# Where a graph network's second layer gets its transposed onehots: turned on TensorE, or compared from keys broadcast by DMA

## The chip, the cores and the metric

One core of a Trainium2 chip runs the whole program. The metric is the device time of one launch in microseconds, without a profile, as a median of several runs.

## What is computed

Two message-passing layers on 12500 nodes with 64 features and 212500 edges, sorted by dst:

```python
h = jnp.maximum(_layernorm(x, axis=-1), 0.0)
x = x + segment_sum(h[src] @ weight[etype], dst)            # layer 0, 16 relations
h = jnp.maximum(_layernorm(x, axis=-1), 0.0)
pre = concatenate([h[src], h[dst], edge_attr]) @ W1 + b1
x = x + segment_sum(relu(pre) @ W2 + b2, dst)               # layer 1
```

All of it is fp32. The text calls the first of these the first layer, the second the second layer.

## The kernel before, in words

The edges are cut into G = 208 groups of 1024, a group into T = 8 tiles of 128 edges. Since dst is sorted, the edges of one tile fall on few neighbouring nodes (at most W0 = 16), those of a group into a window of 128 nodes. A kernel-side test picks a slower path for edge lists where that isn't so; here the fast path runs.

**Gathers.** Either layer needs one table row per edge. POOL issues one indirect DMA per tile (`gather`, L711), 128 rows of 64 numbers each, 8 per group: from x and h_table in the first layer, from p_table in the second. p_table holds every node's h times its part of W1 for src, q_table the same for dst, with b1; both are written during the first layer. POOL's program is an order of its own: it waits once per half-round for the index list `idx`, and before each group until `pre_added` says that the rows of the group two before have been summed.

**Matrices of zeros and ones.** `key1[edge, tile]` is an edge's dst less the first dst of its tile (0 to 15), `key_w[slot]` the place of a slot (tile, offset) in the group's window of nodes. DVE makes, four groups (half a round, B = 4) at a time, `oh1` (edge by slot: `make_onehots`, L1171) and `placer` (slot by node: `make_placers`, L1176), each by one comparison with a row of numbers. The second layer also needs both transposed: `oh1_t` (slot by edge) and `placer_t` (node by slot). Before the change PE turns them (`turn_onehots`, L1394, four transpositions at a time into the PSUM bank `turn_ps`) and ACT copies them to SBUF (`copy_onehots`, L923).

**One group of the second layer.** SP loads a window of q rows (L644). PE picks for each slot its node's q row with placer_t (`pick_q`, L1401), DVE spreads it by tile (`spread_q`, L1211), PE multiplies the edge features by their part of W1 (L1406) and adds oh1_t times q (L1407), DVE adds the gathered p rows (`add_rows`, L1187, which signals `pre_added`), ACT takes the relu (L927), PE sums edges into slots with oh1 (`sum_group`, L1411), DVE keeps each tile's own block and reduces (L1194, L1198), PE places slots into nodes with placer (`place_z`, L1415), and DVE adds that to the accumulator (L1207). `count_edges` (L1182) counts the edges of each slot from oh1_t. The edge features are turned on PE too (`turn_attr`, L1390), which the change leaves as it is.

**Order of the work.** Every engine runs a program written out by hand: a round of U = 8 steps, one group each, in a loop of NIT = 26 rounds. In step u, PE does the products of group u−1, the placement of u−3, the sum of u−2 and the pick of u; DVE the corresponding parts. In steps 1 and 5 DVE makes the onehots of the next half-round, in 2 and 6 the placers; PE turns the onehots in steps 2 and 6 and the placers in 3 and 7; DVE counts in 3 and 7. In step 6 PE also multiplies a finished chunk of nodes by W2 (L1380). SP, in `pairs`, loads q windows for two groups after every second group, and after every fourth the next half-round's `idx` (L637) and edge features `attr` (L628), whose innermost runs are 32 bytes.

**Before the loops.** DVE makes the keys by edge group (`key1_g`, 104 partitions by 2 × 1024) and the places (`head_f`) at 75 to 77 us; PE turns them to the form by edge. The accumulator `acc` lies where the edge lists and `key1_g` lay, and is cleared when they have been read (L1112 to L1114).

## Time and profile before

| | |
|---|---|
| time, median of 3 runs (lowest, highest) | 4229.12 us (4224.97, 4232.71) |
| the profiled execution: its span (the page gives no other time of it) | 5160.7 us |
| POOL busy in the profiled span | 61% |
| PE, DVE, ACT busy | 53%, 29%, 11% |
| granted TensorE clock, mean | 0.681 |
| DMA moved | 144 MB, 28 GB/s |

The execution under the profiler is some 930 us longer than those that are timed. An instruction's duration can be read from it; a wait has to be asked whether it exists without the profiler. The second layer runs from about 2635 us to the end.

### The profile page before, as it was taken

Reading aid. Unit: us, or ns where it says so; the run is one execution under the profiler, and the core shown is the slowest. Engines: PE = TensorE matmul, PEld = TensorE weight load, DVE = VectorE, ACT = ScalarE, POOL = GpSimd, SP = SyncE. Lnnn points to the kernel's source line nnn. Section 1 sums busy time; section 2 is a strip of 40 time slices with the busy share of each in tenths; the row PEclk is TensorE's granted clock in tenths of the full one; section 3 lists DMA queues with packets and bytes.
Section 4 is the critical chain, followed back from the end, with each engine's and each line's share of the span. In section 5 each row is a group of like instructions: output and inputs, shape, how many; then the busy total and the mean of one; then the engine's idle time right before and its main releaser. Section 6 shows DMA issues by size and latency. Waiting matters only on the chain.

```text
span 5160.7 us, 36581 instructions
## 1 busy us (share of the span) xinstructions
PE 2728.2 (53%) x10312; PEld 1524.6 (30%) x10312; DVE 1473.2 (29%) x2000; ACT 582.7 (11%) x1138; POOL 3161.4 (61%) x3350
## 2 busy tenths in 40 slices
PE   2655555555555555455555455554454554554555
PEld 1433333333333333333332222222222222222222
DVE  6322222222222222222233233233232333232232
ACT  3111111111111111111110000010000010000010
POOL 7466565566666566656646566665665666665665
PEclk9776677776767667676766666666666666666666
DMA  4111111111111111111111111111111111111111
GB/s 95 21 24 23 23 26 23 23 26 24 24 25 24 23 24 26 24 23 25 24 27 30 27 29 28 30 30 26 31 29 26 31 30 28 29 29 26 31 29 26
DMA packets 392815, 144.34 MB, mean 28 GB/s; under 512 B 323186, under 2 KB 338859, under 8 KB 392795
## 3 DMA queue, kind: packets, MB, share of 16 engines
q0 software_dynamic: 106496, 109.26, 11.1%
q1 hardware_dynamic: 283685, 34.22, 4.6%
q10 hardware_dynamic: 2614, 0.62, 0.1%
q8 instruction: 8, 0.13, 0.0%
q14 instruction: 12, 0.10, 0.0%
HBM read 129.23 MB, written 12.83 MB: 28 GB/s over the span
## 4 chain that ended last, share of the span: by engine, by line
another core or an unknown queue 33%; PE 24%; issue 21%; POOL 9%; DVE 7%; DVEq 1%; DMA 1%; ACT 1%; SPq 1%; POOLq 0%; ACTq 0%
POOL rows L711 9%; PE ps L1333 7%; PE ps L1407 5%; PE ps L1406 4%; PE ps L1411 2%; DVE q_blk L1211 2%; DVE z_slot L1198 2%; PE ps L1347 2%; PE ps L1340 1%; DVE slots L1187 1%; DVEq L1202 1%; DMA rows<-h_table,idx 1%; PE ps L1306 1%; PE ps L1307 1%
## 5 line engine op out<-in xcount | busy, mean ns | idle before, releaser
L711 POOL DMA_INDIRECT rows<-p_table,idx x1664 | 1574.4, 946 | 959.7 <-issue 527.3
L711 POOL DMA_INDIRECT rows<-h_table,idx x1616 | 1528.2, 946 | 999.0 <-issue 461.4
L1406 PE MATMUL ps<-w_attr,attr_t 64*128 64x512 f32 x416 | 363.2, 968 | 1156.8 <-DVE q_blk L1211 873.1
L1333 PE MATMUL ps<-onehot,rows 128*64 128x256 f32 x3328 | 704.9, 555 | 455.1 <-DMA rows<-h_table,idx 371.2
L1060 DVE TENSOR_TENSOR onehot<-key,ps 128x2048 f32<-128x2048 f32 x209 | 474.1, 2276 | 556.6 <-remote 439.7
L1333 PEld LDWEIGHTS ps<-onehot,rows 128*64 128x64 f32 x3328 | 355.4, 196 | 728.5 <-issue 663.4
L1340 PE MATMUL ps<-w_types,slots 128*128 128x128 f32 x3328 | 455.5, 294 | 96.3 <-issue 78.5
L1340 PEld LDWEIGHTS ps<-w_types,slots 128*128 128x128 f32 x3328 | 424.4, 207 | 151.9 <-issue 131.0
L1187 DVE TENSOR_TENSOR slots<-ps,rows 128x512 f32<-128x512 f32 x208 | 143.9, 692 | 1052.9 <-remote 438.9
L1406 PEld LDWEIGHTS ps<-w_attr,attr_t 64*128 64x128 f32 x416 | 85.9, 256 | 1195.7 <-issue 1195.7
L1407 PE MATMUL ps<-q_blk,onehot 128*128 128x512 f32 x416 | 411.0, 1090 | 0.0
L877 ACT COPY slots<-ps 128x512 f32<-128x512 f32 x416 | 239.9, 587 | 1001.1 <-PE ps L1333 470.4
L1411 PE MATMUL ps<-relus,onehot 128*128 128x512 f32 x416 | 341.3, 918 | 0.0
L927 ACT ACTIVATE relus<-slots 128x512 f32<-128x512 f32 x208 | 131.0, 630 | 1429.8 <-DVE slots L1187 1008.7
L1194 DVE TENSOR_TENSOR z_blk<-ps,blocks 128x512 f32<-128x512 f32 x208 | 143.7, 691 | 494.7 <-remote 280.4
L1347 PE MATMUL ps<-place,nodes_t 128*64 128x256 f32 x416 | 155.3, 513 | 174.5 <-ACT nodes_t L881 138.7
L1127 DVE TENSOR_TENSOR acc<-acc,ps 64x128 f32 x208 | 58.2, 280 | 642.8 <-PE ps L1347 366.3
L1198 DVE TENSOR_REDUCE z_slot<-z_blk 128x64 f32<-128x512 f32 x208 | 208.7, 1003 | 0.0
L1211 DVE TENSOR_TENSOR q_blk<-ps,blocks 128x512 f32<-128x512 f32 x208 | 141.6, 681 | 215.2 <-remote 160.9
L1295 PE MATMUL ps<-ident,stage 64*120 64x64 f32 (+1 forms) x104 | 18.1, 322 | 329.1 <-ACT stage L838 262.2
L1407 PEld LDWEIGHTS ps<-q_blk,onehot 128*128 128x128 f32 x416 | 96.5, 288 | 268.9 <-issue 268.9
L1401 PEld LDWEIGHTS ps<-q_win,onehot 128*128 128x128 f32 x416 | 112.6, 272 | 185.3 <-issue 185.3
(136 smaller groups left out, 1693.0 us busy)
## 6 DMA issues: line engine op xcount, KB each, us to landing
rows<-p_table,idx POOLq DMA_INDIRECT x1664
rows<-h_table,idx POOLq DMA_INDIRECT x1616
attr<-in_edge_attr_dram SPq DMA_DIRECT2D x52, 128.0 KB
q_win<-q_table SPq DMA_DIRECT2D x208, 32.0 KB
p_table<-pq_out SPq DMA_DIRECT2D x25, 120.0 KB
q_table<-pq_out SPq DMA_DIRECT2D x25, 120.0 KB
out_dram<-xs SPq DMA_DIRECT2D x25, 120.0 KB
xs<-in_x_dram SPq DMA_DIRECT2D x6, 480.0 KB, 6.5
```

What stands on the lines that cost most here:

```text
L711: pool.indirect_dma_start(rows[:, u, t, :], None, table, bass.IndirectOffsetOnAxis(ap=idx[:, u, t:t + 1], axis=0)).then_inc(s, 16)
L877: act.copy(to, slot_ps[:, u % 2, t, :].rearrange("p t (r w) -> p t r w", w=W0)).then_inc(slots_copied, 1)
L1060: dve.tensor_tensor(onehot[:, b], key0[:, bass.ds(g, 1), :].rearrange("p a (t c) -> p (a t) c", c=1).broadcast_to([P, T, C0]), iota_ps.rea ...
L1187: dve.tensor_tensor(presum[:, u % 2, 0:T * D], pre_ps[:, u % 2, :], rows[:, u].rearrange("p t d -> p (t d)"), ALU.add).then_inc(pre_added, 1)
L1198: dve.tensor_reduce(z_slot[:, u, 0:D], z_blk[:].rearrange("p (t d) -> p d t", d=D), X, ALU.add).then_inc(z_slotted, 1)
L1211: dve.tensor_tensor(by_tile(q_blk[:, u % 2, :]), q_ps.rearrange("p (a d) -> p a d", a=1).broadcast_to([P, T, D]), own_tile, ALU.mult).then ...
L1333: last = pe.matmul(slot_ps[t % 2 * D:(t % 2 + 1) * D, b, t // 2, :], rows[:, u, t, :], onehot[:, b, t, :], start=True, stop=True)
L1340: last = pe.matmul(nodes_ps, slots[:, b, r, :], w_types[:, r, :], start=(r == 0), stop=(r == R - 1))
L1347: last = pe.matmul(win_ps, nodes_t[:, h * D:(h + 1) * D], place[:, h, :], start=(h == 0), stop=(h == 1))
L1406: pe.matmul(pre_ps[:, u % 2, :], attr_t[half, u // 2, :], w_attr[half].rearrange("k j d -> k (j d)"), start=True, stop=False)
L1407: pe.matmul(pre_ps[:, u % 2, :], oh1_t[:, u, :], q_blk[:, u % 2, :], start=False, stop=True).then_inc(pre_made, 1)
L1411: pe.matmul(z_ps, oh1[:, u, :], relu_rows[:, u % 2, :], start=True, stop=True).then_inc(z_made, 1)
```

## The change

The transposed matrices of the second layer are no longer turned. Early in the first layer SP stores the keys (`key1_g`) and the places (`head_f`) to two new tables in DRAM, `key_rows` and `head_rows`, by nine DMAs, and DVE waits for these before it clears the accumulator. In the second layer SP's new `load_keys` loads for each half-round the four groups' keys straight into `oh1_t`, each tile's row repeated on its 16 partitions, and the places into `placer_t`, repeated on all 128: 256 KB each. These loads count on `attr_in`, as the features do, so each wait for the features (48 in place of 16) is a wait for all three. DVE then compares in place: `oh1_t` with the partition's number modulo 16, `placer_t` with the partition's number (`of_part`, made at the start by an iota on POOL and two small DVE instructions). The semaphore `masks_turned` takes the place of `onehots_copied`, PE and ACT lose the turns and copies, and PE's waits for `onehot1` and `placer1` move to the first use of oh1 and placer in each half-round.

```diff
         SROWS = P * (-(-(N + P) // P))
+        key_rows = dram("key_rows", (G // B, T, B, P), fp32)
+        head_rows = dram("head_rows", (G, P), fp32)
         sums0 = dram("sums0", (SROWS, KA), fp32)
...
         eps = sb("eps", [P, 1], fp32)
+        of_part = sb("of_part", [P, 2], fp32)
+        of_part_i = sb("of_part_i", [P, 2], i32)
         zrows = sb("zrows", [P, D], fp32)
...
         z_ps = ps[:, 2, :]
-        turn_ps = ps[:, 3, :]
         q_ps = ps[:, 4, 0:D]
...
         placer1 = sem("placer1")
-        onehots_turned = sem("onehots_turned")
-        onehots_copied = sem("onehots_copied")
+        tables_stored = sem("tables_stored")
+        masks_turned = sem("masks_turned")
         q_picked = sem("q_picked")
...
                     sp.dma_start(idx[:, u, :], src_tab[:, u, :]).then_inc(idx_in[u], 16)
+                sp.wait_ge(heads_spread, 1)
+                sp.wait_ge(keys_made, 2)
+                for a in range(2):
+                    for b in range(B):
+                        sp.dma_start(key_rows[a * HG // B:(a + 1) * HG // B, :, b, :],
+                                     key1_g[b:HG:B, a, :].rearrange("g (t e) -> g t e", t=T)).then_inc(tables_stored, 16)
+                sp.dma_start(head_rows.rearrange("(a g) e -> g a e", a=2), head_f[:]).then_inc(tables_stored, 16)
...
+                def load_keys(m, k):
+                    of_tile = key_rows[bass.ds(m, 1)].rearrange("n t b e -> t n (b e)").broadcast_to([T, W0, B * P])
+                    sp.dma_start(oh1_t[:, k * B:(k + 1) * B, :].rearrange("p u e -> p (u e)"), of_tile).then_inc(attr_in[k], 16)
+                    of_slot = head_rows[bass.ds(m * B, B), :].rearrange("(a g) s -> a (g s)", a=1).broadcast_to([P, B * P])
+                    sp.dma_start(placer_t[:, k * B:(k + 1) * B, :].rearrange("p u s -> p (u s)"), of_slot).then_inc(attr_in[k], 16)
+
                 def load_idx(g, k):
...
                             if ahead:
+                                load_keys((it + 1) * 2 + k, k)
                                 load_idx((it + 1) * U + k * B, k)
+                            else:
+                                load_keys(0, k)
                             if ahead == 1 and k == U // B - 1:
...
+                sp.wait_ge(tables_stored, 16 * (2 * B + 1))
                 for k in range(U // B):
+                    load_keys(k, k)
                     load_attr(k * B, k)
...
             pool.iota(by_first(slot_row_i[:]), pattern=[[P, 2], [1, P // 2]], base=0, channel_multiplier=0).then_inc(consts_made, 1)
-            pool.wait_ge(consts_made, 10)
+            pool.iota(of_part_i[:], pattern=[[0, 2]], base=0, channel_multiplier=1).then_inc(consts_made, 1)
+            pool.wait_ge(consts_made, 11)
...
-                def copy_onehots(to, n, k):
-                    act.wait_ge(onehots_turned, n)
-                    act.copy(to[:, k * B:(k + 1) * B, :].rearrange("p u c -> p (u c)"), turn_ps).then_inc(onehots_copied, 1)
-
                 def copy_relu(it, u):
...
                         copy_attr(*on(it, u, 2))
-                    if u % B == 2:
-                        copy_onehots(oh1_t, it * 4 + u // B * 2 + 3, (u // B + 1) % 2)
-                    if u % B == 3:
-                        copy_onehots(placer_t, it * 4 + u // B * 2 + 4, (u // B + 1) % 2)
                 copy_attr(0, 0)
-                copy_onehots(oh1_t, 1, 0)
-                copy_onehots(placer_t, 2, 0)
                 for u in range(U):
...
                 tmp, tmp2 = head_rel[:], stat_a[0:HG, NK - 1, 1, 0:2]
-                dve.wait_ge(consts_made, 10)
+                dve.wait_ge(consts_made, 11)
                 chain(dve.tensor_single_scalar(limit_i[:], limit_i[:], U.bit_length() - 1, ALU.arith_shift_right))
...
                     make_onehot0(k - NA - 1, (k - NA - 1) % 2)
+            dve.wait_ge(consts_made, 11)
+            chain(dve.tensor_single_scalar(of_part_i[:, 0:1], of_part_i[:, 0:1], W0 - 1, ALU.bitwise_and))
+            dve.tensor_copy(of_part[:], of_part_i[:])
             chain(dve.tensor_single_scalar(slot_row_i[:], slot_row_i[:], P + W0 - 1, ALU.bitwise_and))
...
                 dve.sem_inc(window_added, AHEAD)
+                dve.wait_ge(tables_stored, 16 * (2 * B + 1))
                 dve.memset(acc[:, 2 * 2 * GE:3 * 2 * GE], 0.0)
...
+                def turn_onehots(n, k):
+                    half = oh1_t[:, k * B:(k + 1) * B, :]
+                    dve.wait_ge(attr_in[k], 48 * n)
+                    dve.tensor_scalar(half, half, of_part[:, 0:1], None, ALU.is_equal).then_inc(masks_turned, 1)
+
+                def turn_placers(k):
+                    half = placer_t[:, k * B:(k + 1) * B, :]
+                    dve.tensor_scalar(half, half, of_part[:, 1:2], None, ALU.is_equal).then_inc(masks_turned, 1)
+
                 def count_edges(n, k):
-                    dve.wait_ge(onehots_copied, n)
+                    dve.wait_ge(masks_turned, n)
                     dve.tensor_reduce(z_slot[:, k * B:(k + 1) * B, D], oh1_t[:, k * B:(k + 1) * B, :], X, ALU.add)
...
                         make_placers(m, k)
+                        turn_onehots(it + 1 + u // B, k)
                     if u % B == 3:
+                        turn_placers(k)
                         count_edges(it * 4 + u // B * 2 + 3, k)
...
                 dve.memset(acc[:], 0.0).then_inc(z_added, AHEAD)
+                turn_onehots(1, 0)
+                turn_placers(0)
                 for u in range(U):
...
                     if u % B == 0:
-                        wait_apart(pe, attr_in[u // B], 16 * (it + 1))
+                        wait_apart(pe, attr_in[u // B], 48 * (it + 1))
                     if not first:
...
-                def turn_onehots(v, k):
-                    for b in range(B):
-                        last = pe.transpose(turn_ps[:, b * P:(b + 1) * P], v[:, k * B + b, :], ident[:])
-                    last.then_inc(onehots_turned, 1)
-
                 def pick_q(it, u):
                     if u % B == 0:
-                        wait_apart(pe, onehots_copied, it * 4 + u // B * 2 + 2)
+                        wait_apart(pe, masks_turned, it * 4 + u // B * 2 + 2)
                     pe.wait_ge(q_in[u % V], 16 * (it * (U // V) + u // V + 1))
...
                     half = slice(u % 2 * T * F, (u % 2 + 1) * T * F)
+                    if u % B == 0:
+                        wait_apart(pe, masks_turned, it * 4 + u // B * 2 + 1)
                     wait_apart(pe, q_spread, it * U + u + 1)
...
                 def sum_group(it, u):
+                    if u % B == 0:
+                        wait_apart(pe, onehot1, it * 2 + u // B + 1)
                     pe.wait_ge(relu_made, AHEAD + it * U + u + 1)
...
                 def place_z(it, u):
+                    if u % B == 0:
+                        wait_apart(pe, placer1, it * 2 + u // B + 1)
                     pe.wait_ge(z_slotted, it * U + u + 1)
...
                         turn_attr(*on(it, u, 2))
-                    k = (u // B + 1) % 2
-                    if u % B == 2:
-                        wait_apart(pe, onehot1, it * 2 + u // B + 2)
-                        turn_onehots(oh1, k)
-                    if u % B == 3:
-                        wait_apart(pe, placer1, it * 2 + u // B + 2)
-                        wait_apart(pe, onehots_copied, it * 4 + u // B * 2 + 3)
-                        turn_onehots(placer, k)
...
                 turn_attr(0, 0, first=True)
-                pe.wait_ge(onehot1, 1)
-                turn_onehots(oh1, 0)
-                pe.wait_ge(placer1, 1)
-                pe.wait_ge(onehots_copied, 1)
-                turn_onehots(placer, 0)
                 for u in range(U):
...
```

## Rows read from the trace of the kernel before

**Rows 1.** the page, parts 1 and 5: busy time by engine, and POOL's gathers
```profile
PE 2728.2 (53%) x10312; PEld 1524.6 (30%) x10312; DVE 1473.2 (29%) x2000; ACT 582.7 (11%) x1138; POOL 3161.4 (61%) x3350
...
L711 POOL DMA_INDIRECT rows<-p_table,idx x1664 | 1574.4, 946 | 959.7 <-issue 527.3
L711 POOL DMA_INDIRECT rows<-h_table,idx x1616 | 1528.2, 946 | 999.0 <-issue 461.4
```

**Rows 2.** line 711 alone: gathers (ns min/median/max), and idle time before them
```profile
L711 POOL DMA_INDIRECT rows<-p_table,idx x1664: 938/944/1478, 2635.5 to 5134.2; - x185
...
  issue: 1002.9, 3128
  DVE slots L1187: 432.3, 79
  PE ps L1333: 303.1, 46
  remote: 208.6, 71
  DMA idx<-src_tab: 25.8, 3
```

**Rows 3.** timeline of POOL, second layer: start us, us, what, idle before
```profile
3902.44 0.94 POOL L711 DMA_INDIRECT rows<-p_table,idx  x1 [0.30 <-issue]
3903.69 0.94 POOL L711 DMA_INDIRECT rows<-p_table,idx  x1 [0.30 <-issue]
```

**Rows 4.** timeline, SP, PE and ACT around one stall of the second layer
```profile
3910.92 0.72 SPq L628 DMA_DIRECT2D attr<-in_edge_attr_dram  x1
...
3919.47 0.28 PE L1390 MATMUL ps<-ident,attr 128*128 128x128 f32 x1
...
3924.39 0.63 ACT L927 ACTIVATE relus<-slots 128x512 f32<-128x512 f32 x1 [15.11 <-DVE slots L1187]
...
3937.69 0.27 ACT L919 COPY attr_t<-ps 128x128 f32<-128x128 f32 x1 [12.67 <-remote]
```

**Rows 5.** timeline of PE: first products of two steps, a turn between
```profile
3936.43 2.04 PE L1406 MATMUL ps<-w_attr,attr_t 64*128 64x512 f32 x2 [16.24 <-issue]
...
3942.72 0.88 PE L1394 MATMUL ps<-ident,onehot 128*128 128x128 f32 x4
...
3945.20 1.09 PE L1406 MATMUL ps<-w_attr,attr_t 64*128 64x512 f32 x2 [1.60 <-DVE q_blk L1211]
```

**Rows 6.** timeline, DVE and POOL together, start and second layer
```profile
73.79 0.29 DVE L1049 CAST iota_f<-iota_i 128x256 f32<-128x256 int32 x1
...
74.19 1.60 POOL L711 DMA_INDIRECT rows<-h_table,idx  x1 [0.30 <-issue]
...
74.46 1.22 DVE L1052 CAST acc<-acc 104x2048 f32<-104x2048 int32 x1
...
2651.36 0.68 DVE L1171 TENSOR_TENSOR onehot<-key,iota_f 128x512 f32<-128x512 f32 x1
...
2651.70 1.16 POOL L711 DMA_INDIRECT rows<-p_table,idx  x1 [0.30 <-issue]
```

**Rows 7.** timeline of the start, and SP's queue from 40 to 50 us
```profile
101.60 0.21 DVE L1074 CAST slot_row<-slot_row_i 1x128 f32<-1x128 int32 x1
...
103.21 1.76 DVE L1112 MEMSET acc<- 128x2048 f32 x1 [1.21 <-issue]
...
110.06 0.94 POOL L711 DMA_INDIRECT rows<-h_table,idx  x1 [13.27 <-DMA idx<-src_tab]
...
q1 hardware_dynamic: 2014, 1.48, 54.4%
```

**Rows 8.** timeline at the handover to the second layer
```profile
2635.48 0.94 POOL L711 DMA_INDIRECT rows<-p_table,idx  x1 [34.40 <-issue]
2635.49 2.89 SPq L628 DMA_DIRECT2D attr<-in_edge_attr_dram  x2
...
2643.95 0.66 PE L1401 MATMUL ps<-q_win,onehot 128*128 128x64 f32 x2 [0.77 <-issue]
...
2649.56 0.69 DVE L1187 TENSOR_TENSOR slots<-ps,rows 128x512 f32<-128x512 f32 x1 [4.23 <-PE ps L1407]
...
2655.66 0.94 POOL L711 DMA_INDIRECT rows<-p_table,idx  x1 [0.30 <-issue]
...
2656.87 0.69 DVE L1187 TENSOR_TENSOR slots<-ps,rows 128x512 f32<-128x512 f32 x1 [4.82 <-DMA rows<-p_table,idx]
```


## The prediction

> **What bounds the kernel now.** I read the page first. It shows POOL busy for 61% of the span, ahead of PE and DVE, and nearly all of that is one instruction, the gather of 128 rows [rows 1]. The next question is whether POOL's other 39% is slack, so I read its idle time by releaser [rows 2]. Of the 1973 us, 1002.9 us lie in 3128 pauses of about 0.30 us each, which follow every gather: one gather starts 1.25 us after the one before it (0.94 busy, 0.30 idle) and nothing is waited for between them [rows 3]. So 3328 gathers (1616 and 1664, and 48 from x) take 3328 × 1.247 = 4150 us by themselves, nearly the whole measured 4229.12.
>
> The rest of the idle time is real waiting, but mostly of the profiled execution alone. All idle time before gathers is 1002.9 + 432.3 + 303.1 + 208.6 + 25.8 = 1972.7 us [rows 2]; the pauses of 0.30 take 3328 × 0.30 = 998; the handover between the layers takes 34 (POOL's idle time ahead of the second layer's first gather [rows 8]) and the first wait for an index list 13 [rows 7]. That leaves 927 us of stalls. The profiled span is 5160.7 us (the page gives no other time of that execution), and 5160.7 − 927 = 4233 us, against a median of 4229.12 without a profile. The two agree within 5 us, so I take the stalls as absent from the runs that are timed. Their look fits: after the edge features' DMA of 32-byte rows is issued, a PE transposition recorded at 3919.47 is answered by ACT's copy of it only at 3937.69, with ACT idle for the last 12.67 us of that [rows 4]. Such a delay belongs to no arithmetic. **So the measured kernel is POOL's row of gathers, with a start, a handover and a tail.** A gather waits for the sum of rows two groups before it, so the other engines have to make a group in 8 × 1.247 = 9.98 us on average. The step with a turn of four placers takes PE 8.77 us from one product to the next, even at its lower granted clock [rows 5]. That is below 9.98, and the two groups of room smooth what is above the mean.
>
> **The change, part by part.**
> Removed: 8 PE transpositions and 2 ACT copies per four groups, with their waits. They lie beside the gathers, in the 1.2 us by which the longest ordinary PE step is shorter than POOL's group [rows 5]. Worth 0. The moved PE waits for onehot1 and placer1 are for DVE work made a half-round earlier: 0.
>
> Added on SP and in the DMA queues, steady state: per four groups two broadcasts of 256 KB, 52 times. They are issued between the q loads and the idx and attr loads of the same half. By the nearest stretch, in which SP's queue moved 1.48 MB within 10 us [rows 7], 512 KB take about 3.5 us. DVE now waits in step 2 or 6 for both tables and the features together. SP issues them when a group's rows are added (step 4), DVE asks at the end of step 6, nearly 2.5 groups or 25 us later. SP's issues (some 6 us), the tables (3.5) and the features (below 5) add up to about 15. Cover 10 us; cost 0. If the cover is gone, DVE stands in the wait with the next group's sum of rows queued behind it, and POOL behind that. The idx load behind the tables has four groups before POOL wants it: 0. A gather's landing behind the broadcasts may come up to 3.5 us later; the room for that is 8 us: the last gather of group 1 ends near 2655.4, its rows are added at 2656.87 [rows 8], and POOL would need that only at 2655.66 + 9.98 = 2665.6. Cost 0.
>
> Added at the start: one more iota on POOL ahead of the first gather, 0.2 us. Two small DVE instructions ahead of the chain heads, first product, idx load, gather, for which POOL stands idle at 110.06; at 0.21 us each [rows 7], 0.4 us. Nine stores (0.85 MB of keys, 0.1 MB of heads) go out from about 77, when the keys are made, need some 7 us at the rate above, and are waited for by DVE only ahead of the memset at 103.21 [rows 7]. Cost 0; from above 3.
>
> Added at the handover: SP issues four table loads of 256 KB ahead of the q loads. The first q pick was at 2643.95, the first sum of rows at 2649.56, and POOL asked for it at 2655.66 [rows 8]. 1 MB more in the queue is 6.9 us: sum of rows done at 2649.56 + 6.9 + 0.69 = 2657.2, which is 1.5 us late. From below 0 (the transfers overlap better), from above 4. I take 1.
>
> Added on DVE: 104 compares of 128x512 against one number per partition, both operands in SBUF. DVE has the time (it is busy 29%). A row of before that is nearest is the CAST, which also has one input: 128x256 in 0.29 us, 104x2048 in 1.22 us, so 512 elements take 0.29 + 256 × (0.93 / 1792) = 0.42 us. But these can cost POOL time, and **this is the term that decides**. The trace shows two kinds of collision [rows 6]. DVE's compare with two SBUF inputs runs from 2651.36 to 2652.04; the gather that starts inside it at 2651.70 takes 1.16 us instead of 0.94 and ends 0.82 after the compare. So a gather needs something in its first 0.12 us that the compare holds. And the CAST from 74.46 to 75.68 starts inside a gather, which normally would end at 75.13 and ends at 75.79, 0.11 after the cast: a one-input instruction of this fast kind also holds what a gather needs in its last 0.11 us. At a random phase a 0.42 us instruction costs 0.30² / (2 × 1.247) = 0.036 at the first place and 0.42² / (2 × 1.247) = 0.071 at the second, 0.107 in all, or 11 us for 104. But the phases aren't random, as DVE's steps begin with the landing of a gather. The 104 two-input compares of 0.68 us in this layer would cost 0.56² / (2 × 1.247) × 104 = 13 us at random, and cost 1574.4 − 1664 × 0.944 = 3.6 us [rows 1, 2]. I take about the same share with something added for a POOL that never stands: 5 us. Bounds: 0, and 104 × 0.42 = 44.
>
> The Trainium skill, "SBUF — State Buffer", section "Who interferes with whom", states a rule on just this: a tensor_scalar or a cast in a two-port mode contends with GpSimd's descriptor making, and whichever starts first holds the port pair for its whole length. The rows agree that there is contention, but the cast of 74.46 did not wait for the gather that had begun at 74.19, so the second half of the rule isn't seen. By the rule as written, only compares that begin in the 0.30 us pause would stretch a gather: an estimate of 0.24 × 104 × at most 0.42 = 10 us.
>
> Sum: 0.2 + 0.4 + 1 + 5 = 6.6 us. On the profiled execution's own stall-free sum that is 4233 → 4240; on the median it gives 4229.1 + 6.6, **4236 us**.
>
> **The rivals.**
> *The compares lock POOL out nearly every time* (slower). Same mechanism, larger share: since DVE's order is tied to POOL's landings, the phase may be the bad one in each of the 104. Place: the turned placers and onehots at the ends of steps 2, 3, 6, 7. For it: no row shows this instruction and POOL is never idle in the timed runs. Against it: the present compares pay a quarter of the random price. It decides from a mean of 0.07 us a compare on, (8.5 − 1.6) / 104. Its price is up to 44 us: about 4230 + 40 = 4270.
> *The compares hold nothing* (same). If this form runs in the slow mode with one input, as the reduction and the sums from PSUM do, it costs no gather anything: 4229 + 1.6 = 4231.
> *The tables land late* (slower). If the broadcast, which reads one row for many partitions, moves at a third of the rate above, the 10 us of cover are used up; each us beyond is paid 52 times, 2 us give 104, 4335. Against it: 2 KB rows are longer than those of most loads here.
> *Stalls exist without the profile, and the turns cause part of them* (faster). For it: the mean granted clock is 0.681, and the sixth step, with the turn and the output product, is longer than the others. Against it: the 4233 above leaves no room. If such steps overran by 0.7 us once in each of 26 rounds, 18 us would go and 1.6 come: 4213.
>
> **How the numbers follow.** A measurement of this kernel tells apart about 0.2%, 8.5 us. The forecast has 0.46: sums from 4231 to 4245, of which 0.34 lie within 8.5 us and 0.12 above. The compares hold nothing: 0.12, same. POOL locked out: 0.18, slower. Tables late: 0.10, slower. Turns mattered: 0.14, faster. So faster 0.14, same 0.46, slower 0.40. The range from 4212 to 4272 holds all but the late tables and the outer parts of the first and the last rival.
>
> **What would show it.** Right: POOL's gathers in the second layer still 1.25 us apart; the count of gathers above 0.97 us up, with the new compares beside them; the new compare at 0.42 us; busy of L711's second group up by about 5 us; ACT's and PE's idle time longer by what was removed. Wrong: if DVE is seen idle ahead of the onehots' compare, released by the table's DMA, the tables are late; if the gathers' mean rises above 0.960 us, POOL is locked out; if the time falls by more than 8.5 us with the gathers as before, the stall-free reading of the timed runs is false.

## The result, and the profile after

The changed kernel takes 4257.61 us (median of 4, 4247.39 to 4260.02), the kernel before 4229.41 (median of 4, 4224.97 to 4232.71): a ratio of 1.0060, 95% interval 1.0047 to 1.0072. It is 0.6% slower, by 28 us. Measured once more beside the experiments it was 4247.55 against 4222.29, ratio 1.0058 (1.0044 to 1.0072), so 25 us. The page below is that of the shortest of the first four executions, 4247.39 us; the other three took 4257.51 to 4260.02, none of them was profiled, and what made them 10 us longer stays open.

First the page of the changed kernel, parts 1 and 5. Line numbers have moved: L733 is the gather (L711 of before), L1212 the sum of rows (L1187 of before). In the changed kernel L1187 and L1192 are the older two comparisons, which make the onehots and the placers (L1171 and L1176 of before), and L1199 and L1203 are the new two, for the turned onehots and the turned placers.

```profile
span 4245.6 us, 35885 instructions
...
PE 2586.1 (61%) x9888; PEld 1467.2 (35%) x9888; DVE 1496.0 (35%) x2108; ACT 518.4 (12%) x1032; POOL 3179.3 (75%) x3351
```

```profile
L733 POOL DMA_INDIRECT rows<-p_table,idx x1664 | 1594.1, 958 | 539.8 <-issue 532.6
L733 POOL DMA_INDIRECT rows<-h_table,idx x1616 | 1527.1, 945 | 495.5 <-issue 477.9
...
L1212 DVE TENSOR_TENSOR slots<-ps,rows 128x512 f32<-128x512 f32 x208 | 143.9, 692 | 1321.8 <-DMA rows<-p_table,idx 1311.7
```

The span is 4245.6 us and POOL's two groups of gathers hold 3121 us of it. Their idle time is 539.8 and 495.5, nearly all "issue", the pauses of 0.30 us, against 959.7 and 999.0 in [rows 1]: this execution has none of the stalls of the profile of before. ACT and PE have lost their turns, and nobody gained by it. Of the idle time ahead of DVE's sum of rows, 1311.7 of 1321.8 us are waits for the gathers' landing.

The mean gather of the second layer takes 958 ns, where [rows 1] had 946. The comparisons, by line and form, from 2300 to 4200 us (47 half-rounds; count, busy us, mean ns):

```profile
L1187 DVE TENSOR_TENSOR onehot<-key,iota_f 128x512 f32<-128x512 f32 x47 | 31.6, 672 | 0.0
...
L1199 DVE TENSOR_SCALAR onehot<-onehot,of_part 128x512 f32<-128x512 f32 x47 | 22.4, 476 | 0.0
L1203 DVE TENSOR_SCALAR onehot<-onehot,of_part 128x512 f32<-128x512 f32 x47 | 22.3, 475 | 0.0
```

The new ones take 0.476 us, not the 0.42 worked out from the casts. The start and the handover, on POOL's timeline (start, duration, idle time before):

```profile
98.39 0.94 POOL L733 DMA_INDIRECT rows<-h_table,idx  x1 [3.31 <-DMA idx<-src_tab]
```

```profile
2148.86 0.94 POOL L733 DMA_INDIRECT rows<-p_table,idx  x1 [1.70 <-DVE slots L1212]
```

At the start POOL waits 3.31 us for an index list. The kernel before waits 2.79 there (e10, below):

```profile
98.56 0.94 POOL L711 DMA_INDIRECT rows<-h_table,idx  x1 [2.79 <-DMA idx<-src_tab]
```

But this wait differs by more than that from run to run: it is 2.06 in the changed kernel of e9, and 4.06 in e8, which has nothing of the change. A cost of the start isn't shown. Ahead of the third group of the second layer POOL waits 1.70 us (1.62 in e9), where e10 has only the pause of 0.30: the first sum of rows is late by about what was forecast.

### The profile page after: what moved, and what is told of

It reads as the page before. It is cut to its first block, busy times and chain, and to the rows that moved or that the text cites. A ratio compares the mean times of both kernels' runs of the same rounds, so it can differ in the third digit from the quotient of the medians.

```text
span 4245.6 us, 35885 instructions
## 1 busy us (share of the span) xinstructions
PE 2586.1 (61%) x9888; PEld 1467.2 (35%) x9888; DVE 1496.0 (35%) x2108; ACT 518.4 (12%) x1032; POOL 3179.3 (75%) x3351
## 4 chain that ended last, share of the span: by engine, by line
POOL 62%; issue 27%; PE 4%; DMA 4%; DVE 1%; SPq 1%; POOLq 0%; ACT 0%; ACTq 0%; DVEq 0%
POOL rows L733 62%; PE ps L1362 3%; DMA rows<-h_table,idx 2%; DMA rows<-p_table,idx 1%; DVE slots L1212 0%; SPq L565 0%; PE ps L1369 0%; SPq L542 0%; SPq L546 0%; POOLq L360 0%; DMA q_win<-q_table 0%; PE ps L1433 0%; PE ps L1432 0%; SPq L560 0%; DVE stat_a L1035 0%
## 5 line engine op out<-in xcount | busy, mean ns | idle before, releaser
L733 POOL DMA_INDIRECT rows<-p_table,idx x1664 | 1594.1, 958 | 539.8 <-issue 532.6
L733 POOL DMA_INDIRECT rows<-h_table,idx x1616 | 1527.1, 945 | 495.5 <-issue 477.9
L1362 PE MATMUL ps<-onehot,rows 128*64 128x256 f32 x3328 | 632.1, 544 | 721.5 <-DMA rows<-h_table,idx 721.1
L1432 PE MATMUL ps<-w_attr,attr_t 64*128 64x512 f32 x416 | 403.2, 1069 | 784.3 <-DVE q_blk L1236 784.3
L1212 DVE TENSOR_TENSOR slots<-ps,rows 128x512 f32<-128x512 f32 x208 | 143.9, 692 | 1321.8 <-DMA rows<-p_table,idx 1311.7
L1369 PE MATMUL ps<-w_types,slots 128*128 128x128 f32 x3328 | 442.6, 296 | 0.0
L1433 PE MATMUL ps<-q_blk,onehot 128*128 128x512 f32 x416 | 427.6, 1131 | 0.0
L1432 PEld LDWEIGHTS ps<-w_attr,attr_t 64*128 64x128 f32 x416 | 96.1, 286 | 815.2 <-issue 815.2
L1445 PEld LDWEIGHTS ps<-onehot,z_slot 128*65 128x65 f32 x416 | 96.5, 232 | 240.5 <-issue 232.2
L1445 PE MATMUL ps<-onehot,z_slot 128*65 128x128 f32 x416 | 131.4, 420 | 5.2 <-DVE z_slot L1223 5.2
```

The lines of the kernel that those rows point to most:

```text
L733: pool.indirect_dma_start(rows[:, u, t, :], None, table, bass.IndirectOffsetOnAxis(ap=idx[:, u, t:t + 1], axis=0)).then_inc(s, 16)
L1212: dve.tensor_tensor(presum[:, u % 2, 0:T * D], pre_ps[:, u % 2, :], rows[:, u].rearrange("p t d -> p (t d)"), ALU.add).then_inc(pre_added, 1)
L1362: last = pe.matmul(slot_ps[t % 2 * D:(t % 2 + 1) * D, b, t // 2, :], rows[:, u, t, :], onehot[:, b, t, :], start=True, stop=True)
L1369: last = pe.matmul(nodes_ps, slots[:, b, r, :], w_types[:, r, :], start=(r == 0), stop=(r == R - 1))
L1432: pe.matmul(pre_ps[:, u % 2, :], attr_t[half, u // 2, :], w_attr[half].rearrange("k j d -> k (j d)"), start=True, stop=False)
L1433: pe.matmul(pre_ps[:, u % 2, :], oh1_t[:, u, :], q_blk[:, u % 2, :], start=False, stop=True).then_inc(pre_made, 1)
```

## The experiments

Theory: nothing that was taken away bounded anything, and the 25 to 28 us are gathers stretched by DVE's comparisons. Rival: the stores, the loads and the waits cost it. "The port" is a short name for what a comparison and a gather can't have at the same time; a gather counts as stretched when it takes over 0.97 us in place of 0.944. The eight experiments that are compared with 4222 us were run beside the kernel before in three series, its medians 4222.89 (e5), 4222.29 (e6 to e9) and 4222.37 (e10 to e12).

### e1 to e4: a chip on which the same program takes 5185 us

e1 is the kernel before, unchanged.

> The kernel before, unchanged: how far two programs with the same instructions differ, and whether a second profile has the stalls of the first. If the stalls are the profiler's, the timed ratio is 1.000 and the profile may come out near 4230 us with POOL's gathers 1.25 us apart; their time in the second layer then gives what the two comparisons with two SBUF inputs cost without stalls (3.6 us in the first profile; 9 us in the profile of the change). If the stalls were real, the profiled span stays near 5160 us.

e2 is the change with the comparisons' second operand in PSUM:

```diff
+        part_ps = ps[:, 3, P:P + 2]
...
+                chain(dve.tensor_copy(part_ps, of_part[:]))
                 make_onehots(0, 0)
...
-                    dve.tensor_scalar(half, half, of_part[:, 0:1], None, ALU.is_equal)
+                    dve.tensor_tensor(half, half, part_ps[:, 0:1] (over B and P), ALU.is_equal)
```

> The change, but its two comparisons take the partition's number from PSUM, so that each has one SBUF input and can't run in the fast two-port form. Port theory: they stretch no gather, although each takes 0.69 us in place of 0.48; the time falls by 15 to 25 us from the change's 4257.6, to 4233 to 4242, and the gathers next to them take 0.94 us. Rival, the tables' DMAs or the start cost the 28 us: the time stays at 4255 to 4262.

e3 is the kernel before with the change's stores, loads and waits:

```diff
+                for a in range(2):
+                    for b in range(B):
+                        sp.dma_start(key_rows[...], key1_g[...])
...
+                                load_keys((it + 1) * 2 + k, k)      # into unused columns of presum
                                 load_idx((it + 1) * U + k * B, k)
...
-                        wait_apart(pe, attr_in[u // B], 16 * (it + 1))
+                        wait_apart(pe, attr_in[u // B], 48 * (it + 1))
```

> The kernel before, with all of the change's DMAs and waits (the nine stores, DVE's wait for them, the two 256 KB loads per half-round, into SBUF that nothing reads, PE's wait for them), while the matrices are turned on PE as before. Port theory: 4229 to 4233, at most 3 us for the start and the handover. Rival, DMA: 4250 to 4260.

e4 is the change with each new comparison followed by one more:

```diff
                     dve.tensor_scalar(half, half, of_part[:, 0:1], None, ALU.is_equal).then_inc(masks_turned, 1)
+                    dve.tensor_scalar(unused_b, unused_a, of_part[:, 0:1], None, ALU.is_equal)
```

> The change, with each of its two comparisons followed by a second one of the same form (128x512, one SBUF input, into SBUF that nothing reads), so 208 in place of 104. Port theory: the pair takes some 0.88 us in a row, and an instruction that starts in it or ends in it waits: 10 to 40 us more than the change, 4268 to 4298. Rival, DMA or start: the same as the change within 3 us, since DVE has the time (35% busy).

On this chip the kernel before took 5185.52 us (median of 29, 5068.35 to 5239.79), without a profile. The ratios were 0.9987 (0.9902 to 1.0072) for e1, 1.0021 (0.9959 to 1.0082) for e2, 1.0102 (1.0000 to 1.0204) for e3 and 1.0050 (0.9994 to 1.0106) for e4. The gathers of line 711 in e1's profile, with their idle time by releaser:

```profile
L711 POOL DMA_INDIRECT rows<-p_table,idx x1664: 938/944/1497, 2593.0 to 5192.6; - x185
...
  issue: 996.6, 3127
  DVE slots L1187: 528.7, 79
  PE ps L1333: 273.5, 49
  remote: 204.1, 68
```

These are the stalls of [rows 2], 528.7 and 273.5 and 204.1 us where that had 432.3, 303.1 and 208.6. So they aren't the profiler's: on this chip every execution has them, and the first profile had them with a span of the same size. By that span the first profile would come from such a chip, and the times beside it from one without; no run shows this directly. Where POOL stands 1000 us, gathers longer by 25 us (0.5%) can't be told from noise: the intervals of e2 and e4 reach from below 1 to above 1.005, that of e3 from 1.0000 to 1.0204. These three say nothing for or against the theory. What makes the stalls, these runs leave open.

### e5: the new comparisons without the port

The kernel of e2, where the kernel before takes 4223 us.

> The same kernel as e2_new_psum (the change's two comparisons take the partition's number from PSUM). On the chip of e1 to e4 every execution took over 5000 us, with POOL standing some 460 us in each layer, so gathers a little longer couldn't show. Where the kernel before takes 4230 us, port theory: 4233 to 4242, no gather stretched by L1200 or L1204. Rival (DMA or start): 4255 to 4262. If the kernel before takes over 5000 us again: no difference that can be told.

4234.12 us (4228.35 to 4236.52), ratio 1.0028 (1.0018 to 1.0039), in the range of the port theory. The page's row of gathers, and a stretch of the timeline with the new comparison (L1205, 0.67 us long) between two gathers, the first of which it covers at its end:

```profile
L735 POOL DMA_INDIRECT rows<-p_table,idx x1664 | 1578.8, 949 | 538.5 <-issue 532.5
```

```profile
3041.47 0.94 POOL L735 DMA_INDIRECT rows<-p_table,idx  x1 [0.30 <-issue]
3041.88 0.67 DVE L1205 TENSOR_TENSOR onehot<-onehot,ps 128x512 f32<-128x512 f32 x1
...
3042.72 0.94 POOL L735 DMA_INDIRECT rows<-p_table,idx  x1 [0.30 <-issue]
```

The gather of 3041.47 ends at 3042.41, inside the comparison, and has its ordinary 0.94 us. No gather is stretched by the new comparisons. The 32 long ones, 8.8 us in all, end 0.82 us after an older comparison. The changed kernel's new comparison is 0.2 us shorter and costs some 14 us more (25.3 and 11.2 above the kernel before). So more than half of the cost is the form of the new comparison and where its operand lies, not how long it takes. 11 us are left.

### e6: the tables alone

> The same kernel as e3_tables_only (the kernel before with all of the change's stores, loads and waits, turned on PE as before). e5 left 11 us of the change's cost (4234.1 against 4222.9 of the kernel before in the same job) when its two comparisons stretched no gather. If these 11 us are the start, the handover and the DMAs: 8 to 12 us above the kernel before. If they are the two older comparisons at another phase: within 3 us of it.

4235.29 us, ratio 1.0030 (1.0018 to 1.0042): 13 us, with no comparison added at all. By time alone this is nearest the first of the two readings, and 1 us above its range. The profile decides against it:

```profile
L732 POOL DMA_INDIRECT rows<-p_table,idx x1664 | 1580.7, 950 | 538.3 <-issue 533.1
```

The gathers are busy 1580.7 us, 10.5 more than in the kernel before (e10). Of those over 0.97 us, 33 end 0.82 us after an onehots' comparison with two SBUF inputs, an old one, which these cost 10.2 us; the placers' cost 0.5. So of the 13 us about 11 are stretched gathers here too, and 2 or 3 are left, of which the handover is 1.5 (POOL waits 1.79 ahead of the third group). How loads can do this is seen below, with e9 and e10.

### e7: no comparison holds the port

e5's kernel, and the older two comparisons read the row of numbers from PSUM too:

```diff
+                chain(dve.tensor_copy(iota_q, iota_f[:, 0:P]))      # PSUM bank 3
...
-                                      iota_f[:, 0:W0] (over B * T), ALU.is_equal).then_inc(onehot1, 1)
+                                      iota_q[:, 0:W0] (over B * T), ALU.is_equal).then_inc(onehot1, 1)
```

> The change, with all four comparisons' second operand in PSUM, so that none of them has two SBUF inputs or the two-port form. In e5's profile the older two still cost 8.8 us. Port theory: no gather of the second layer above 0.97 us but the first few, and 8 to 10 us less than e5: 4225 to 4227 where the kernel before takes 4223 to 4229. Rival (DMA, start): as e5, 11 us above the kernel before.

4222.49 us, ratio 1.0003 (0.9994 to 1.0012). That is 11.6 us below e5, more than the 8 to 10 expected, and below the range of 4225 to 4227.

```profile
L735 POOL DMA_INDIRECT rows<-p_table,idx x1664 | 1570.0, 944 | 540.5 <-issue 531.5
```

No gather of the second layer takes over 0.97 us. All DMAs of the change are still there, and all of PE's turns still gone, and the whole costs nothing and gains nothing that can be told (its wait ahead of the third group, 2.24 us, is still there). This is the version to keep if the change is wanted; it doesn't beat the kernel before.

### e8: the older comparisons at another place in the step

```diff
                         add_window(*back(it, u, 3))
+                    if u % B == 1:
+                        make_onehots(m, k)
+                    if u % B == 2:
+                        make_placers(m, k)
                     if not first or u >= 2:
                         reduce_z(*back(it, u, 2))
                     spread_q(it, u)
-                    if u % B == 1:
-                        make_onehots(m, k)
-                    if u % B == 2:
-                        make_placers(m, k)
```

> The kernel before, with make_onehots and make_placers (two SBUF inputs, 0.68 us) moved within DVE's step from behind spread_q to behind add_window. By the phases of the change's profile a step's DVE work begins 0.06 to 0.1 us after a gather starts; the comparison would then run from 1.5 to 2.2 us, clear of the first 0.12 us of each gather (at 1.25 and 2.5). Phase theory: 3 to 12 us faster than the kernel before. If the phase isn't locked: the same within 2 us. Against it: reduce_z and spread_q come 0.6 us later, which PE's slack of 1 us a step should hide.

Missed: 4246.90 us, ratio 1.0056 (1.0042 to 1.0069), 25 us slower with the kernel before's own instructions, only reordered. The gathers of the page, and one collision:

```profile
L711 POOL DMA_INDIRECT rows<-p_table,idx x1664 | 1593.8, 958 | 538.4 <-issue 538.1
```

```profile
3029.90 1.56 POOL L711 DMA_INDIRECT rows<-p_table,idx  x1 [0.30 <-issue]
3029.96 0.68 DVE L1171 TENSOR_TENSOR onehot<-key,iota_f 128x512 f32<-128x512 f32 x1
```

The comparison begins 0.06 us after the gather, and the gather ends 0.82 after it: 1.56 us. All 104 comparisons begin inside a gather, 0.04 to 0.32 us after its start. The 36 that begin up to 0.141 us after it stretch it, by some 0.65 us each, or 24 us; the 68 that begin from 0.144 us on stretch none. So the short need at a gather's start is over after 0.14 us. I had expected the comparison about 0.25 us after a gather's start; it comes at 0.17 in the median, and that tenth is what it turns on. It shows the strength of the mechanism better than the run it was meant to be: a phase alone is worth 0.6%.

### e9 and e10: the change and the kernel before, both without stalls

> The change itself, beside the others: 4250 to 4258, 0.6% above the kernel before.

> The kernel before, unchanged, for a profile without stalls. e7 (no comparison can hold the port) timed equal to it, so its two comparisons should stretch hardly a gather: second-layer gathers busy 1566 to 1570 us against 1576.9 with the same comparisons in e6. If they cost 9 us here too, e7 owes its time to something else that is slower by 9 us.

e9: 4247.55 us, 2.5 below the range expected. e10: 4222.35 us, ratio 1.0001 (0.9991 to 1.0010). The gathers of the second layer, e9 and then e10:

```profile
L733 POOL DMA_INDIRECT rows<-p_table,idx x1664 | 1596.8, 960 | 539.8 <-issue 534.8
```

```profile
L711 POOL DMA_INDIRECT rows<-p_table,idx x1664 | 1570.2, 944 | 538.5 <-issue 538.2
```

26.6 us between the two, for 25.2 us between the times. (For e6 the row above has 1580.7, not the 1576.9 of e10's expectation.) The profiled executions took 4250.02 and 4222.23: 27.8 us, of which 26.6 are these gathers and 1.3 the wait ahead of the third group; the second layer's first gather starts at 2127.43 and 2127.53. The kernel before without stalls has one gather above 0.97 us there, stretched by 0.2. Its timeline, in a step with an onehots' comparison:

```profile
3016.53 0.94 POOL L711 DMA_INDIRECT rows<-p_table,idx  x1 [0.30 <-issue]
3017.74 0.69 DVE L1187 TENSOR_TENSOR slots<-ps,rows 128x512 f32<-128x512 f32 x1 [6.98 <-DMA rows<-p_table,idx]
...
3020.66 0.68 DVE L1171 TENSOR_TENSOR onehot<-key,iota_f 128x512 f32<-128x512 f32 x1
...
3021.52 0.94 POOL L711 DMA_INDIRECT rows<-p_table,idx  x1 [0.30 <-issue]
```

The sum of rows (L1187) begins 0.03 us before a gather, the comparison (L1171) ends at 3021.34, and the next gather begins at 3021.52. It clears by 0.18 us here. Over the 52 half-rounds the median is 0.13, from 0.03 to 0.28, and in one the gather is hit. Now the change, in the three steps with comparisons:

```profile
3030.26 0.69 DVE L1212 TENSOR_TENSOR slots<-ps,rows 128x512 f32<-128x512 f32 x1 [7.67 <-DMA rows<-p_table,idx]
...
3033.20 0.67 DVE L1187 TENSOR_TENSOR onehot<-key,iota_f 128x512 f32<-128x512 f32 x1
...
3033.42 1.26 POOL L733 DMA_INDIRECT rows<-p_table,idx  x1 [0.30 <-issue]
...
3042.95 0.68 DVE L1192 TENSOR_TENSOR onehot<-key_w,iota_f 128x512 f32<-128x512 f32 x1
...
3043.54 0.48 DVE L1199 TENSOR_SCALAR onehot<-onehot,of_part 128x512 f32<-128x512 f32 x1
3043.72 1.12 POOL L733 DMA_INDIRECT rows<-p_table,idx  x1 [0.30 <-issue]
...
3052.64 1.06 POOL L733 DMA_INDIRECT rows<-p_table,idx  x1 [0.30 <-issue]
3053.11 0.47 DVE L1203 TENSOR_SCALAR onehot<-onehot,of_part 128x512 f32<-128x512 f32 x1
```

Three things go wrong. The onehots' comparison, 3033.20 to 3033.87, now lies over the start of the gather of 3033.42, which takes 1.26 us. The new onehots' comparison (L1199) is put behind the placers' and lies over the start of the gather of 3043.72: 1.12 us. The new placers' comparison (L1203) begins inside the gather of 3052.64 and ends at 3053.58; the gather ends 0.12 later, at 3053.70, after 1.06 us. Counted by which comparison a long gather ends behind, e9 has 11.3 us from L1187, 9.9 from L1199 (52 gathers), 5.1 from L1203 (49) and 0.4 from L1192, 26.7 in all. L1187 hits 37 gathers.

Why does the first, an instruction of the old kernel, collide at all? The sum of rows of 3030.26 begins 2.15 us after its group's last gather ends, where all the others take 1.5 to 1.6: over the 52 groups of this step the median is 2.20 in e9, 2.25 in e6 and 1.57 in e10, and in the other three steps 1.54 to 1.59 in all of them. That is what puts the comparison past the next gather's start. SP's queue in e9 (issue, start and duration), and the busy share of the DMA engines from 3018 to 3032 in 40 slices of 0.35 us, tenths:

```profile
3022.15 0.71 SPq L648 DMA_DIRECT2D onehot<-key_rows  x1
3023.07 0.33 SPq L650 DMA_DIRECT2D onehot<-head_rows  x1
...
3024.31 0.43 SPq L638 DMA_DIRECT2D attr<-in_edge_attr_dram  x1
```

```profile
DMA  0040003004012621447669899999994881300040
```

The group's last gather ends at 3028.11, in the 29th slice, amid the burst of the tables and features. The same for e10 from 3005 to 3019, where the features are issued at 3010.98 and the last gather ends near 3016.2, in the 32nd slice, after the burst:

```profile
DMA  0040041005003103623278799999304100400410
```

The features' 4096 packets of 32 bytes were there before; the tables in front of them push them by some 3 us onto the last gather's landing. Which packets hold the landing up isn't separated by any run; that the loads do it is shown by e6, which of the change has only them, the stores and the waits. That the later start of the step comes from the later landing is read from these two profiles and wasn't tested apart.

### e11: only the older two from PSUM

> The change, with only its two older comparisons on a PSUM operand; the two new ones are as in the change. Port theory, with the shares read in e9's profile (9.9 and 5.1 us for the new ones, 11.7 for the older): 4222 plus 12 to 18, so 4234 to 4240, second-layer gathers busy near 1581 us. If the two kinds don't add up: either 4222 or 4247.

4238.15 us, ratio 1.0038 (1.0023 to 1.0052), 15.8 us above the kernel before.

```profile
L735 POOL DMA_INDIRECT rows<-p_table,idx x1664 | 1582.5, 951 | 539.5 <-issue 533.5
```

Predicted 12 to 18. The excess of the gathers is 7.7 us from the new onehots' comparison and 4.9 from the new placers'. With e5's 11.2 us for the old ones that makes 27.0, and the change has 25.3: the two kinds add up.

### e12: two comparisons in a row

> The same kernel as e4_double (each new comparison followed by one more of its form). Port theory, where POOL doesn't stand: with the pair 0.9 us long, 10 to 40 us above the change's 4247.6, so 4258 to 4288, and gathers beside it of up to 1.9 us. If only the first instruction at a phase counts: 4247.

4253.19 us, ratio 1.0075 (1.0061 to 1.0089). That is 5.6 us above e9, less than the 10 I had as the least.

```profile
L733 POOL DMA_INDIRECT rows<-p_table,idx x1664 | 1600.5, 962 | 541.2 <-issue 533.7
```

```profile
3048.04 0.48 DVE L1203 TENSOR_SCALAR onehot<-onehot,of_part 128x512 f32<-128x512 f32 x1
3048.30 1.03 POOL L733 DMA_INDIRECT rows<-p_table,idx  x1 [0.30 <-issue]
3048.44 0.48 DVE L1198 TENSOR_SCALAR slots<-slots,of_part 128x512 f32<-128x512 f32 x1
```

The pair (L1203, and the second at L1198) lies from 3048.04 to 3048.92, and the gather of 3048.30 ends at 3049.33, which is 0.81 after the end of the first, not of the second. That isn't always so. The same step of an earlier round:

```profile
3007.35 0.48 DVE L1203 TENSOR_SCALAR onehot<-onehot,of_part 128x512 f32<-128x512 f32 x1
3007.61 1.43 POOL L733 DMA_INDIRECT rows<-p_table,idx  x1 [0.30 <-issue]
3007.74 0.48 DVE L1198 TENSOR_SCALAR slots<-slots,of_part 128x512 f32<-128x512 f32 x1
```

Here the second ends at 3008.22 and the gather at 3009.04, 0.82 after the second: both have held it. Of the 51 gathers whose start an onehots' pair covers, 34 end 0.82 after the first comparison and cost 5.1 us; 17 end 0.82 after the second, take up to 1.77 us and cost 10.5. What decides between the two, no run shows. A pair at a gather's end is another matter: the 46 gathers that the placers' pair hits there end 0.12 after its first comparison, while the second runs. So both of the expectation's readings are half right. The sum stays low because the older onehots' comparison hits 27 gathers here for 8.3 us, where e9 has 37 and 11.3: its phase has moved as well. The gathers' busy time is 3.7 us above e9's, 1600.5 against 1596.8.

## Why the prediction was right and where it failed

4257.61 us lies in the range of 4212 to 4272, but 21 us above the 4236 of the forecast. A difference of 28 us is over three times the 8.5 us that the prediction counts as told apart, so by its own measure the kernel is slower, which it gave 0.40, and not the same, which it gave 0.46.

**POOL's gathers bound the kernel: right.** Against e10 and its time, all seven other runs from e5 on differ by what their second-layer gathers are busy longer, to within 4 us (the worst is e11: 12.3 and 15.8).

**"I take the stalls as absent from the runs that are timed": right for the runs that were timed, wrong in its cause.** The conclusion was sound, but I put the stalls down to the profiler. e1 to e4 have them without it. The sum of 4233 also took the first wait for an index list, 13 us, as real; e10 has 2.79, so most of it was a stall too, and the sum comes to some 4223, where e10's span is 4220.5. On that chip the change could hardly have been told: e4, which contains it, has a ratio of 1.0050 (0.9994 to 1.0106).

**The turns "lie beside the gathers ... Worth 0": right.** e7 has lost them and takes 4222.49 us where the kernel before takes 4222.29. The faster rival falls with that.

**Handover 1: right. Start 0.6: not shown.** The wait ahead of the third group is 1.4 us longer in the first profile and 1.3 in e9. The wait at the start varies between 2.06 and 4.06 us over e8, e9 and e10, and the second layer starts at the same time in e9 and e10. In e7's time neither can be seen.

**"A gather's landing behind the broadcasts may come up to 3.5 us later ... Cost 0": this step failed first.** The sum of rows that follows the landing comes 0.6 us later in one step of four, well within the room for POOL's own wait, as argued. But DVE's whole step hangs on that landing. The step begins later against the row of gathers, and a comparison that cleared the next gather by 0.13 us in the median now lies over its start in 37 half-rounds of 52. It measured 11 us (e6, and 11.3 in e9). I priced a wait and not a phase, though the phase was what my own largest term hung on. No rival and no bound had this cost; that the range still held the time is luck, as its upper end was set by another rival's 44 us, of which only 15 came.

**"About the same share ... 5 us": the term was mis-sized.** It measured 15.0 us in e9 (9.9 and 5.1), and 12.6 in e11. The two kinds of collision and their 0.82 and 0.11 us were right (0.82 and 0.12 measured), and are the whole of it. What failed is that the older comparisons' share was carried over to the new ones. The share belongs to a place in DVE's step: without stalls each new comparison meets the gather at the same place in nearly every round, 52 and 49 times of 52, while the older two, at their places in e10, hit one gather of the layer. So a profile of the kernel before without stalls would have misled me further, to a share of nearly 0. The random price, 11 us, would have been the better number, and the upper bound of 44 was the right one to keep in the range. The instruction's length was 0.48 for 0.42.

From e10's profiled execution to e9's, 4222.2 + 1.3 + 15.0 + 11.7 (the older two) = 4250.2, against 4250.0. On 4229 the same terms give 4257, the first median, but the one execution of that measurement that was profiled took 4247. The result is between the forecast and the rival that POOL is locked out (0.18), whose mechanism it is at a third of its full price; the mean of 0.14 us for each new comparison is past its deciding point of 0.07, and the sign that I had set for it, gathers above 0.960 us in the mean, stands at its bound, 0.958 and 0.960. Tables late: no; DVE never waits for them.

**Whichever starts first holds the port: seen in one direction only.** The Trainium skill, "SBUF — State Buffer", section "Who interferes with whom", says that a VectorE instruction with at most one SBUF input, outside the two-port modes, doesn't contend with GpSimd. e5 and e7 agree: with the operand in PSUM no gather is stretched by it. The same section says that whichever starts first holds the pair for its whole length. Where the comparison starts first, that is what the rows show: the gather of 3043.72 in e9 ends 0.82 after it. Where the gather starts first, it isn't: L1203 starts inside a gather and runs its ordinary 0.47 us, and in e8 a comparison that starts 0.06 us after the gather delays it. The rows show two short needs of a gather, one in its first 0.14 us (e8) and one in its last 0.12; a comparison with two SBUF inputs was seen to hold only the first.

## What to carry to other kernels

Where POOL issues gathers without a pause and sets the time, look at every VectorE instruction beside it with two SBUF inputs or with the fast one-input form, and count the gathers that it stretches. Where there are some, give it an operand in PSUM: e7 against e9 is 25 us for that alone. The kernel before, with one stretched gather of its second layer (0.2 us), has nothing of this to win. A transfer that is "hidden" still moves the step that starts with it, so in a kernel whose engines run in step a phase has a price as a wait has. And before a profile's idle time is explained, add it up against the timed median: here that sum told that a fifth of the profile wasn't in the timed runs, though not why.

## What the runs showed that I had not expected

The same program takes 4222 us on two chips and 5185 on a third (5068 to 5240 in 29 executions), with POOL standing in both layers. The order of two comparisons among others on VectorE, with no dependency touched, is worth 25 us in 4222 (e8). And a gather whose start a comparison covers is held by a second comparison directly behind the first in 17 cases of 51, and in 34 it isn't (e12).
